# A changed opening: small vectors over another queue, one load moved up, the first mixer product ahead of the shift's chain

## The reference, cut to what matters

```
mod = (silu(c) @ wmod).reshape(2, 6, 1, 512)           # c: 2 x 512, wmod: 512 x 3072
sa, ca, ga, sb, cb, gb = mod[:, 0..5]                   # shift, scale, gate; twice
h  = layernorm(x) * (1 + ca) + sa                       # x: 2 x 1024 x 512
# attention block
g       = sigmoid(gate)
x_shift = roll(h, -512 rows) @ Wts.T * g + h * (1 - g)
xn      = layernorm(x_shift) * ln_w + ln_b
k, v    = xn @ Wk.T, xn @ Wv.T                          # 64 wide
s_t     = s_(t-1) * exp(time_decay) + exp(-exp(time_first) * sigmoid(k)) * v
x       = x + ga' * (states @ Wo.T)
h       = layernorm(x) * (1 + cb) + sb
x       = x + gb' * moe(h)      # router, shared expert of 1408, 32 experts, top 4, capacity 64
```

## Time and profile before

| | us |
|---|---|
| median of 3 runs | 723.08 |
| the runs | 720.56, 723.08, 728.20 |
| the profiled execution, its own time | 720.62 |
| its span, first to last instruction | 718.8 |
| TensorE busy | 672.5 (94%) |
| VectorE busy | 365.5 (51%) |
| ScalarE busy | 288.6 (40%) |
| GpSimd busy | 184.4 (26%) |
| mean granted TensorE clock | 0.976 |

### The profile page before, as it was taken

The page is one execution under the profiler, slowest core; times in us unless marked ns, Lnnn a source line. Parts: engine busy times, 40 slices in busy tenths (PEclk is TensorE's granted clock), DMA queues, the critical chain, the costliest instruction groups (busy, mean ns, idle before and its releaser), DMA issues.

```text
span 718.8 us, 8895 instructions
## 1 busy us (share of the span) xinstructions
PE 672.5 (94%) x3218; PEld 467.9 (65%) x3218; DVE 365.5 (51%) x714; ACT 288.6 (40%) x552; POOL 184.4 (26%) x174
## 2 busy tenths in 40 slices
PE   4898788999998899998999899999999999999997
PEld 3665456768576667887665566666666666667875
DVE  3768759679687887763124223122122243225755
ACT  3444775656656543323234224233232343323231
POOL 1254465554627200000112122222221222120000
PEclk9799987999999999999999999999999999999999
DMA  7760200000223006305777877778899787816311
GB/s 276 243 238 1 76 15 30 16 30 18 85 77 116 29 1 232 134 1 206 267 235 231 291 229 261 249 234 282 270 324 338 239 273 258 284 23 234 117 50 69
DMA packets 50295, 118.27 MB, mean 165 GB/s; under 512 B 6904, under 2 KB 11084, under 8 KB 50252
## 3 DMA queue, kind: packets, MB, share of 16 engines
q1 hardware_dynamic: 45388, 109.31, 43.0%
q0 software_dynamic: 4864, 8.40, 5.4%
HBM read 100.87 MB, written 18.91 MB: 167 GB/s over the span
## 4 chain that ended last, share of the span: by engine, by line
PE 61%; DVE 5%; DMA 3%; ACT 2%; issue 2%; POOL 2%; SPq 0%; DVEq 0%; ACTq 0%; POOLq 0%
PE bank L1690 28%; PE bank L1702 11%; PE bank L1745 11%; PE bank L1762 6%; DMA egu<-in_L_ffn_Wu_dram 1%; PE bank L1733 1%; ACT xsH L860 1%; DMA xg<-h_rows,slot_tok 1%; PE bank L1793 1%; PE bank L1751 1%; DVE xres L1260 1%; DVE prodL L1224 1%; POOL ho L634 1%; DVE prod L1222 1%; POOL xres L642 1%
## 5 line engine op out<-in xcount | busy, mean ns | idle before, releaser
L1690 PE MATMUL bank<-xsH,wguH 128*128 128x512 f32 x352 | 144.1, 409 | 1.5 <-DVE xsL L1214 1.1
L1690 PE MATMUL bank<-xsL,wguH 128*128 128x512 f32 x352 | 138.9, 394 | 0.0
L1690 PE MATMUL bank<-xsH,wguL 128*128 128x512 f32 x352 | 138.6, 394 | 0.0
L1690 PEld LDWEIGHTS bank<-xsH,wguH 128*128 128x128 f32 x352 | 67.0, 190 | 25.5 <-issue 10.9
L1222 DVE TENSOR_TENSOR prod<-bank,silu 128x512 f32<-128x512 f32 x38 | 26.2, 690 | 111.2 <-PE bank L1690 87.7
L1745 PE MATMUL bank<-egu,xeT 128*64 128x352 f32 x512 | 79.3, 462 | 3.1 <-DMA egu<-in_L_ffn_Wu_dram 2.6
L1702 PE MATMUL bank<-wdH,prodH 128*128 128x512 f32 x176 | 73.7, 419 | 6.4 <-DVE prodL L1224 4.2
L692 POOL DMA_INDIRECT expert_sums<-ye,slot_to x32 | 49.4, 1543 | 115.7 <-DMA expert_sums<-ye,slot_to 91.5
L1690 PEld LDWEIGHTS bank<-xsL,wguH 128*128 128x128 f32 x352 | 66.9, 190 | 14.8
L1690 PEld LDWEIGHTS bank<-xsH,wguL 128*128 128x128 f32 x352 | 66.8, 190 | 13.2 <-issue 0.7
L699 POOL DMA_INDIRECT xg<-h_rows,slot_tok x16 | 16.8, 1053 | 219.8 <-DVE slot_w L1368 90.0
(11 more groups left out here) (222 smaller groups left out, 1019.8 us busy)
## 6 DMA issues: line engine op xcount, KB each, us to landing
egu<-in_L_ffn_Wg_dram SPq DMA_DIRECT2D x32, 704.0 KB, 6.0
egu<-in_L_ffn_Wu_dram SPq DMA_DIRECT2D x32, 704.0 KB, 7.5
ed<-in_L_ffn_Wd_dram SPq DMA_DIRECT2D x32, 512.0 KB, 5.3
h2T<-in_L_wmod_dram SPq DMA_DIRECT2D x6, 1024.0 KB, 8.9
ed<-in_L_ffn_Wd_dram SPq DMA_DIRECT2D x32, 192.0 KB, 6.3
h_rows<-ho SPq DMA_DIRECT2D x16, 256.0 KB, 2.0
expert_sums<-ye SPq DMA_DIRECT2D x16, 256.0 KB, 8.8
out_dram<-xres SPq DMA_DIRECT2D x16, 256.0 KB, 2.2
```

What stands on the lines that cost most here:

```text
L1690: ins = mm.matmul(bk[:, :], l[f][:, w, c, :], r[:, c, :], start=(k == 0), stop=(k == 3 * C - 1))
```

## The change

The six small loads and their wait for the zeroed rows go from SyncE to the head of ScalarE's stream. On SyncE's queue block 0 of wmod (the scale) moves ahead of the two single tiles of x. A new semaphore `ca_ok` parts the scale from the shift: VectorE takes the scale's columns as soon as `vector_columns(0)` is done, then makes 1 + ca, K_A and the low parts 0 and 1, and only then the shift's columns, `saT`, `tmpc` and the low parts 2 and 3. TensorE has product 0 and its columns ahead of the turn of `h` 0, and `mixer(0)` leaves the loop: its chunks 0 to 2 stand ahead of product 2, chunk 3 behind it, columns 2 and the spreads after that. ScalarE's order follows. Left out below is the declaration of the semaphore.

```diff
@@ -452,13 +452,6 @@
 
             @block.sync
             def _(sp):
-                sp.wait_ge(rows_zero, 1)
-                for src, r in ((gate, GATE), (ln_w, LNW), (ln_b, LNB)):
-                    sp.dma_start(rows[r:r + C, :], src.rearrange("(c p) -> c p", p=P)).then_inc(cols_in, 16)
-                sp.dma_start(rows[CC:CC + B * C, :], c_in.rearrange("b (c p) -> (b c) p", p=P)).then_inc(cols_in, 16)
-                for src, r in ((time_decay, TD), (time_first, TF)):
-                    sp.dma_start(rows[r:r + 1, 0:S], src.rearrange("(a s) -> a s", a=1)).then_inc(cols_in, 16)
-
                 def load_mod(j):
                     sp.dma_start(stage[STAGE[j]], wmod_v[:, :, BLOCK[j] * 512:(BLOCK[j] + 1) * 512]).then_inc(stage_in[STAGE[j]], 16)
 
@@ -467,9 +460,9 @@
                     sp.dma_start(xres[:, lo:hi, :], x_rows[:, lo:hi, :]).then_inc(x_in[b * 2 + h], 16)
 
                 sp.dma_start(stage[0], Wts.rearrange("(c p) d -> p c d", p=P)).then_inc(stage_in0, 16)
+                load_mod(0)
                 for k, i in enumerate((HB, 0)):
                     sp.dma_start(xres[:, i, :], x_rows[:, i, :]).then_inc(x_first[k], 16)
-                load_mod(0)
                 load_mod(1)
                 load_x(0, 1, 1)
                 sp.dma_start(kvN[0:S, :], Wk).then_inc(kv_in, 16)
@@ -793,7 +786,7 @@
                     a.activation(partial[:, n % 2, :], partb[n % 2][:, :], ACT.Copy).then_inc(part_ok, 1)
 
                 def scale_weights(b, chunks=range(C)):
-                    act.wait_ge(sa_ok, 1)
+                    act.wait_ge(ca_ok, 1)
                     for c in chunks:
                         if b:
                             if c < C - 1:
@@ -922,20 +915,26 @@
                             if j + 1 < NP:
                                 pair_rows(j + 1)
 
+                act.wait_ge(rows_zero, 1)
+                for src, r in ((gate, GATE), (ln_w, LNW), (ln_b, LNB)):
+                    act.dma_start(rows[r:r + C, :], src.rearrange("(c p) -> c p", p=P)).then_inc(cols_in, 16)
+                act.dma_start(rows[CC:CC + B * C, :], c_in.rearrange("b (c p) -> (b c) p", p=P)).then_inc(cols_in, 16)
+                for src, r in ((time_decay, TD), (time_first, TF)):
+                    act.dma_start(rows[r:r + 1, 0:S], src.rearrange("(a s) -> a s", a=1)).then_inc(cols_in, 16)
                 act.wait_ge(col_ok, 1)
                 a.activation(ecol[:, 0:C], cols[:, GATE:GATE + C], ACT.Exp, scale=-1.0).then_inc(exp_ok, 1)
                 a.activation(ecol[:, C:C + B * C], cols[:, CC:CC + B * C], ACT.Exp, scale=-1.0).then_inc(exp_ok, 1)
                 a.activation(wcol[:, 0:2], cols[0:S, TD:TD + 2], ACT.Exp).then_inc(exp_ok, 1)
                 for q in range(C):
                     take(("wts", q))
+                part_out(0)
                 take(("h", 0))
-                part_out(0)
-                part_out(1)
                 for q in range(C):
                     turn_taken(act, ("wts", q))
                 scale_weights(0, [0])
+                part_out(1)
+                scale_weights(0, [1, 2, 3])
                 part_out(2)
-                scale_weights(0, [1, 2, 3])
                 take(("spread", 0, K_A))
                 take(("spread", 0, K_B))
 
@@ -1058,8 +1057,8 @@
                     v.tensor_tensor(hT[:, n % 2, 1, :, :], bank[k][:, :].rearrange("p (c m) -> p c m", c=C),
                                     hT[:, n % 2, 0, :, :].bitcast(F32), ALU.subtract).then_inc(t_taken[k], 1)
 
-                def scale_weights(b):
-                    for c in range(C):
+                def scale_weights(b, chunks=range(C)):
+                    for c in chunks:
                         dve.wait_ge(wts_hi, b * C + c + 1)
                         v.scalar_tensor_tensor(wtsL[:, c, :], wtsT[:, c, :], dcol[:, b, K_1CA, c:c + 1],
                                                wtsH[:, c, :].bitcast(F32), ALU.mult, ALU.subtract).then_inc(wts_lo, 1)
@@ -1092,17 +1091,19 @@
                     first_stats(0, i)
                     first_var(k)
                 first_rows(HB)
+                used(dve, M_CA)
+                link(v.tensor_copy(modc[:, 0, :, :].rearrange("p c b -> p (c b)"), modp(0, 1)))
+                v.tensor_scalar(dk(K_1CA), modc[:, M_CA, :, :], 1.0, None, ALU.add).then_inc(ca_ok, 1)
                 first_rows(0)
                 h_lo(0)
-
+                dve.wait_ge(ca_ok, 1)
+                link(v.tensor_tensor(dk(K_A), dk(K_1CA), g1, ALU.mult))
+                scale_weights(0, [0, 1])
                 used(dve, M_SA)
-                link(v.tensor_copy(modc[:, 0:2, :, :].rearrange("p j c b -> p (j c b)"), modp(0, 2)))
-                link(v.tensor_copy(saT[:, :, 0:B], modc[:, M_SA, :, :]))
-                v.tensor_scalar(dk(K_1CA), modc[:, M_CA, :, :], 1.0, None, ALU.add).then_inc(sa_ok, 1)
-                dve.wait_ge(sa_ok, 1)
-                link(v.tensor_tensor(dk(K_A), dk(K_1CA), g1, ALU.mult))
+                link(v.tensor_copy(modc[:, 1, :, :].rearrange("p c b -> p (c b)"), modp(1, 1)))
+                v.tensor_copy(saT[:, :, 0:B], modc[:, M_SA, :, :]).then_inc(sa_ok, 1)
                 link(v.tensor_tensor(tmpc[:, 0, :, :], modc[:, M_SA, :, :], g1, ALU.mult))
-                scale_weights(0)
+                scale_weights(0, [2, 3])
                 used(dve, "wsa")
                 v.tensor_tensor(dk(K_B), modb[:, WSA_AT:WSA_AT + C * B].rearrange("p (c b) -> p c b", c=C),
                                 tmpc[:, 0, :, :], ALU.add).then_inc(spread_ok, 1)
@@ -1629,11 +1630,13 @@
                         pe.wait_ge(s_taken[k], n)
                     return k
 
-                def mixer(t):
-                    k = product_bank(("mixer", t))
-                    turn_taken(pe, ("h", t))
-                    hi, lo, n = hT[:, t % 2, 0, :, :], hT[:, t % 2, 1, :, :], 0
-                    for c in range(C):
+                def mixer(t, chunks=range(C)):
+                    k, _ = product_at(("mixer", t))
+                    if 0 in chunks:
+                        product_bank(("mixer", t))
+                        turn_taken(pe, ("h", t))
+                    hi, lo, n = hT[:, t % 2, 0, :, :], hT[:, t % 2, 1, :, :], 3 * chunks[0]
+                    for c in chunks:
                         if t % BT == 0:
                             pe.wait_ge(wts_lo, t // BT * C + c + 1)
                         for l, r in ((hi, wtsH), (hi, wtsL), (lo, wtsH)):
@@ -1641,7 +1644,8 @@
                             n += 1
                         if t == BT - 1 and c < C - 1:
                             ins.then_inc(w_read, 1)
-                    ins.then_inc(s_full[k], 1)
+                    if C - 1 in chunks:
+                        ins.then_inc(s_full[k], 1)
 
                 def keys_values(g):
                     k = product_bank(("kv", g))
@@ -1796,12 +1800,14 @@
 
                 for q in range(C):
                     turn(("wts", q))
+                vector_product(0)
+                vector_columns(0)
                 turn(("h", 0))
-                vector_product(0)
                 vector_product(1)
-                vector_columns(0)
                 vector_columns(1)
+                mixer(0, [0, 1, 2])
                 vector_product(2)
+                mixer(0, [3])
                 vector_columns(2)
                 turn(("spread", 0, K_A))
                 turn(("spread", 0, K_B))
@@ -1811,7 +1817,7 @@
                     r = router_group(t)
                     for q in before_mixer(t):
                         turn(q)
-                    if t < NT:
+                    if 0 < t < NT:
                         mixer(t)
 
                     new_states = t == 13
```

More of the change, by code:

```diff
@@ L257, in build @@
          xn_ok, ho_ok, h2_ok, h2_sent0, h2_sent1, h2_sent2, e_tanh, e_fac, st_ok,
-         vef_ok, vex_ok, veh_ok, rsf_ok, rsx_ok, rsh_ok, dve_self, pool_self,
+         vef_ok, vex_ok, veh_ok, rsf_ok, rsx_ok, rsh_ok, dve_self, pool_self, ca_ok,
          vrows_out, ab_in, cb_in, sb_in, rg_in, gate_in) = sems(
@@ L264, in build @@
              "xn_ok ho_ok h2_ok h2_sent0 h2_sent1 h2_sent2 e_tanh e_fac st_ok "
-             "vef_ok vex_ok veh_ok rsf_ok rsx_ok rsh_ok dve_self pool_self "
+             "vef_ok vex_ok veh_ok rsf_ok rsx_ok rsh_ok dve_self pool_self ca_ok "
              "vrows_out ab_in cb_in sb_in rg_in gate_in")
```

## The result

| | before | changed |
|---|---|---|
| median of 20 runs each | 723.00 us | 726.37 us |
| lowest and highest | 720.11, 728.20 | 722.25, 730.95 |
| ratio | 1 | 1.0051, 95% interval 1.0033 to 1.0070 |
| profiled execution, its span | 720.62, 718.8 | 727.02, 725.2 |

The change makes the kernel 3.4 us slower, 0.5%. That lies within the 1% named in the prediction, but outside its range (717.8 to 725.0) and on the other side of its direction. The same kernel measured again later gave 725.82 against 723.10, ratio 1.0051 (1.0022 to 1.0080).

The account below looks back on a forecast made before the run. Everything later was taken to hang on VectorE's first `mix_front`: `K_B` 0.27 us later, a 1.13 wait gone, so 0.86 less. That gave 720.62 - 0.86 = 719.8 profiled, 721.85 - 0.86 = 721.0 as median, range 717.8 to 725.0.

Parts of the forecast that it names:

- the sum's term for the small loads beside the large ones: Opening, ScalarE's queue: small vectors 0.5 us later beside large loads, columns at 4.5, scaling of `Wts` at 6.8.
- rival 1: Small vectors stand behind large loads on the shared DMA engines, columns at 5.4 or later; chance 0.13.
- its two prices: Late columns: behind `Wts` +0.9 us, 721.5 on the profiled scale; behind the scale weights too, +3.6, 724.2.
- The chain from there to the first `mix_front`: Opening: scaling at 6.8, `K_B` at 23.95, first `mix_front` at 33.25 against 34.11, 0.86 us less.
- the turn of `h`, priced at 1.06: TensorE in the opening, behind `vector_columns(0)`: the turn takes 1.06 us, to 15.9.
- That `K_B` would wait for TensorE and not for low weights: VectorE at `K_B`, near 23.95: waits for TensorE, since the last low chunk ends near 21.
- the harmless move of the table load: ScalarE: the 1.28 us table load moves behind the six issues, ends at about 4.2 and costs nothing.
- A cost of the second place of the scale weights: SyncE's queue: block 0 ahead of two row tiles; no loss unless the tiles come 1.5 us late.
- "What is late next is VectorE itself": Behind `K_B`: the bias is ready early, its 1.13 us wait goes, and VectorE's statistics and row tiles are late next.
- The scale of the median: Median of new runs without the change taken as 721.85 us, the middle of 720.62 and 723.08.
- Rival 2: TensorE's clock falls inside the new opening: `K_B` at 25.8, +1.0 us, 721.6; chance 0.14.
- Rival 3: `Wts` is earlier but the third product's chain, VectorE's stretch or another ring wait uses it up: 720.6; chance 0.16.

Follow-up runs that it names:

- e3: Changed kernel, with SyncE's first large load held until the six small loads on ScalarE's queue have landed; 725.32 against 722.47 us before, ratio 1.0042.
- e9: Changed kernel, with SyncE issuing `Wts` as it does but everything behind it only after the six small loads have landed; one run of 725.36 us.
- e4: Changed kernel, with VectorE's two kv bias copies moved ahead of the third and fourth tiles' normalized rows; 723.69 against 722.47 us before.
- e2: Changed kernel, with the six small loads back at the head of SyncE's queue, so the new order alone; 723.89 against 722.47 us before, ratio 1.0017.
- e6: Changed kernel, with the small loads back on SyncE's queue and the kv bias copies moved up; 722.61 against 722.73 us before, ratio 1.0004.
- e10: Changed kernel measured again without edits; 725.82 against 723.10 us before, ratio 1.0051.
- e1: Kernel before, with only the six small loads and their wait moved from SyncE to ScalarE's queue; 723.29 against 722.47 us before, ratio 1.0010.

## Why the prediction was wrong

**The step that failed** is the sum's term for the small loads beside the large ones: "I take 0.5 us more, nearer to the quiet end ...; columns at 4.5". It measured 3.7 (7.74 against 4.00), or 4.87 us from the last issue where the quiet engines take 1.33. The scaling of `Wts` began at 9.91 instead of the forecast 6.8. This is rival 1, which had 0.13, and it came out between its two prices (behind `Wts`, and behind the scale weights too). The reason given for the low value, that the vectors are few and in a queue of their own, is what e3 and e9 refute: in e9 none of their packets moved for a whole microsecond while `Wts` did. The rule cited beside it, from the Trainium skill (DMA: Bandwidth & Descriptors, section Queues, rings and completion order), that each engine takes packets in turn from the queues that have work, does not foretell this wait: 8 of e9's small packets did move beside `Wts`, then none from 4 to 5 (whether the others were in the engines' queues by then isn't shown). The measurement decides. The term's upper bound did reach far enough (724.2 on the profiled scale), but the likeliest value and the weight did not. The range's end of 725.0 does not follow from its terms either: 724.2 and the 2.5 of scatter make 726.7.

**The chain from there to the first `mix_front` held.** Forecast from scaling to `K_B` 17.15 us, measured 17.04 (9.91 to 26.95); from `K_B` on 9.30, measured 9.54, with the wait for the bias gone. The forecast `mix_front` was 0.86 earlier, the measured one 2.38 later; of the 3.24 between them 3.11 are the late columns. That the 17.15 came out to 0.1 is in part luck. The first vector product took 1.35 instead of 1.06 and its columns started 0.4 us later after the scaling than forecast; the turn of `h`, priced at 1.06, took 0.64 and gave it back. Most of both comes from the clock: the row of 1.06 for that turn was taken at the half level, which the prediction did not see, and the first vector product began at it. That `K_B` would wait for TensorE and not for low weights and the harmless move of the table load (ended at 4.46, first exponential at 8.26) came as said. A cost of the second place of the scale weights does not show: their load was in before the first vector product began.

**A second step failed:** "What is late next is VectorE itself". That is true at the first `mix_front`, but not up to the fifth. The prediction saw that the bias products come early without the mixer between; it did not ask who waits for VectorE's copies of them. `vector_columns(3)` does, because it writes the same bank, and with the mixer gone TensorE has nothing else: 3.48 us idle, 1.81 instead of 1.02 for the columns, the second mixer product 2.9 us later (38.73 against 35.84). The mixer's products are then what `mix_front` waits for, and the shift grows from 2.38 to 3.64. e4 (1.4 us back) and e2 with e6 (61.39 against 58.55) show that it goes with the copies' place.

The idle needs the half clock to cost that much. Five executions have it at 3.47 or 3.48 us: e9, e10, e3, the changed kernel, e2. Their shift grows by 0.13, 0.93, 0.98, 1.26 and 1.67 us between the first and the fifth `mix_front`. In the same order grows the time from the start of the second mixer product to the clock's return: 2.0, 3.8, 3.9, 4.4 and 5.3 us. In e4, where that product starts at 37.07, 4.6 us of half clock come behind its start and the shift even shrinks by 0.3; the kernel before has its own at half clock for the most part too (0.50 granted from 36 to 38). So neither the idle nor the clock costs this much alone. From the fifth on the shift holds to the tenth (114.94 against 111.33, 3.6), which is near the measured 3.4; behind the tenth the profiled executions part by 2.8 us more, which nothing here explains.

**The scale of the median.** I set 721.85 for a median of before; 20 runs gave 723.00, 1.2 more. With the right scale, the forecast would still have been 722.1 and the direction wrong.

**Rival 2** (the clock falls inside the new opening) did not happen where it was put: in the changed kernel 1.00 was granted from 16 up to 36. A fall came behind it, at the end of the idle that the change made (0.67 in the window from 36). The kernel before has one at 35 without that idle (0.67 in the window from 35), but is back at 1.00 from 39 on, the changed kernel only in the window from 43 (0.92); what makes it longer no run isolates. In e1 the clock did fall in the opening, and that cost 1.4 us in two rows. What the prediction had wrong of the clock is the opening's first turns, which ran at half (last section). Rival 3 is what e6 shows for the new order once its idle is filled.

## What to carry to other kernels

A few small loads that the first step needs must be through before the first large load moves data; a queue of their own does not carry them past it, and half of them on each of two queues, all issued before the large one, brought the columns to 3.3 to 3.5 us instead of 4.0. When a product is moved forward into a busy stretch, look at the stretch it leaves: an idle engine there waits for the next thing in its stream, here a bank that another engine frees late, and with the half clock of TensorE behind it that cost 0.1 to 1.7 us from one execution to another. Put work ahead only of what is not on the chain to the last event; mixer chunks ahead of the third vector product cost 1.6 to 1.7 us at `K_B`, and behind the spreads they filled time in which TensorE had nothing to do. Before a row of TensorE is used as a price, compare it with the same work elsewhere: it may have been taken at half clock.

## What was not expected of the hardware

Small loads on ScalarE's queue (256 bytes to 4 KB each) took 4.87 us from the last issue to the use beside 1 MB loads of SyncE's queue, and 1.37 without them (e3, from 2.81 to 4.18). The waiting came behind the issues, which ran at their pace.

TensorE turns `Wts` at half clock, though the windows print 1.00 there. The window of the earlier trace rows and all others of the first microseconds say 1.00, but these traces hold no clock record that early: the first, of the full level, begins at 14.9 us in the kernel before, at 15.9 in the changed one, and between 12.4 and 17.8 in the others. The rows tell the level ahead of it. The same 16 turns take 3.67 us at 11.63 in the changed kernel and 2.02 at 27.27, where 1.00 is granted; in the kernel before they take 3.68 at 10.32 and 3.75 at 24.00, where 0.50 is granted, in the stretch that begins with the fall of the earlier trace rows. So the turns of `Wts` ran at 1.2 GHz in both. What the level was while TensorE stood idle before them, no row tells. The rise came while TensorE turned `Wts` or `h` or multiplied the first vector, or just behind that, at another time in each execution, even of one kernel. What it is worth is the first vector product: 1.94 us where the rise comes behind it, 1.06 or 1.07 where it comes ahead.
